# Two edge loops of a graph network on Trainium2: no memsets between the gathers of the additive loop, its turn and sums at later lags; in the attention loop the merge moves to VectorE, a copy to ScalarE, and GpSimd only gathers

## What is computed

```python
# layer 1, "additive": 4 heads of 32 channels
projected = (x @ W).reshape(N, 4, 32)
scores = tanh(projected[row] + projected[col])
scores = einsum('ehc,hc->eh', scores, att)
scores = exp(scores - max(scores, axis=0))
out = segment_sum(projected[row] * scores[:, :, None], col)
out = out / maximum(segment_sum(scores, col), 1e-12)[:, :, None]

# layer 2, "GAT": 2 heads of 128 channels
e = leaky_relu(xl[src] + xr[dst], 0.2)
alpha = einsum('ehd,hd->eh', e, att)
alpha = exp(alpha - segment_max(alpha, dst)[dst])
alpha = alpha / (segment_sum(alpha, dst)[dst] + 1e-16)
out = segment_sum(xl[src] * alpha[..., None], dst).mean(axis=1) + h @ res_W + bias
```

## Time and profile before

| | |
|---|---|
| time, median of 3 runs | 4551.61 us (4547.66 to 4561.69) |
| the profiled execution | 4548.06 us, of which the span is 4546.3 us |
| busy over the span | PE 87%, DVE 63%, ACT 39%, POOL 73% |
| gathers of the additive layer | from 672.23 to 1862.8 us |
| gathers of GAT | from 1981.62 to 3100.7 us |
| granted clock over the span | 0.877 |

### The profile page before, as it was taken

The page is one execution under the profiler, slowest core; times in us unless marked ns, Lnnn a source line. Parts: engine busy times, 40 slices in busy tenths (PEclk is TensorE's granted clock), DMA queues, the critical chain, the costliest instruction groups (busy, mean ns, idle before and its releaser), DMA issues. The chain is left out here.

```text
span 4546.3 us, 91170 instructions
## 1 busy us (share of the span) xinstructions
PE 3966.6 (87%) x22715; PEld 2253.3 (50%) x22818; DVE 2873.2 (63%) x8482; ACT 1768.1 (39%) x4516; POOL 3334.8 (73%) x4366
## 2 busy tenths in 40 slices
PE   2998848889898888679999999996799999999977
PEld 1344434455455555445555554554465656656552
DVE  7997033333333333567677776776788888888859
ACT  3775033444434444343333333333322222222217
POOL 0533238888888888468888888884588888888862
PEclk8999977777767777689898999998899999999999
DMA  2222622222222222044333333331566666666650
GB/s 86 82 83 66 200 76 62 59 59 58 58 59 57 59 59 57 21 148 116 111 111 111 112 111 111 111 111 28 103 103 105 104 104 104 104 105 104 105 102 14
DMA packets 377441, 402.57 MB, mean 89 GB/s; under 512 B 86457, under 2 KB 322502, under 8 KB 377030
## 3 DMA queue, kind: packets, MB, share of 16 engines
q0 software_dynamic: 151904, 198.72, 22.8%
q1 hardware_dynamic: 225382, 202.21, 15.7%
HBM read 312.91 MB, written 87.78 MB: 88 GB/s over the span
## 5 line engine op out<-in xcount | busy, mean ns | idle before, releaser
L1735 POOL DMA_INDIRECT sums<-gathered,idx x606 | 988.9, 1632 | 217.4 <-issue 166.1
L896 POOL DMA_INDIRECT gathered<-table,sources x952 | 917.6, 964 | 169.6 <-issue 134.3
L1597 PE MATMUL bank<-wide 128*128 128x512 bf16 x3533 | 829.2, 379 | 5.6 <-issue 0.2
L2411 ACT ACTIVATE msg<-bank,neg_top 80x512 f32<-80x512 f32 (+1 forms) x404 | 275.9, 683 | 858.1 <-DVE neg_top L2465 842.9
L1597 PEld LDWEIGHTS bank<-wide 128*128 128x128 bf16 x3636 | 347.7, 98 | 364.1 <-issue 1.8
L2463 DVE TENSOR_REDUCE neg_raw<-bank 80x1 f32<-80x512 f32 (+1 forms) x404 | 276.7, 685 | 388.9 <-PE bank L2341 328.5
L896 POOL DMA_INDIRECT wide<-table,sources x464 | 447.9, 965 | 76.9 <-issue 62.3
L1236 POOL TENSOR_TENSOR acc<-acc,msg 128x20 f32 x404 | 172.8, 428 | 350.2 <-issue 188.4
L2320 PE MATMUL bank<-ident,gathered 128*128 128x128 f32 x1360 | 277.9, 322 | 140.8 <-DMA gathered<-table,sources 118.2
L2320 PEld LDWEIGHTS bank<-ident,gathered 128*128 128x128 f32 x1360 | 188.9, 162 | 412.4 <-issue 197.1
L2341 PE MATMUL bank<-zact,att_cells 128*80 128x512 f32 x404 | 319.9, 886 | 0.0
(11 more groups left out here) (413 smaller groups left out, 8006.8 us busy)
## 6 DMA issues: line engine op xcount, KB each, us to landing
zact<-in_src_flat SPq DMA_DIRECT2D x202, 192.0 KB, 3.1
edge_rows<-in_attr_rows SPq DMA_DIRECT2D x202, 128.0 KB
dst_pair<-local_rows SPq DMA_DIRECT2D x177, 128.0 KB
gathered<-table,sources POOLq DMA_INDIRECT x952, 2.6
dst_pair<-local_rows SPq DMA_DIRECT2D x202, 64.0 KB
counts<-wide SPq DMA_DIRECT2D x4, 3000.0 KB
counts<-fm_ab SPq DMA_DIRECT2D x4, 3000.0 KB
fm_ab<-counts SPq DMA_DIRECT2D x4, 3000.0 KB, 11.2
```

Of the source, the lines that this page charges most:

```text
L896: pool.indirect_dma_start(out=g[:, j, :], out_offset=None, in_=table, in_offset=bass.IndirectOffsetOnAxis(ap=mine, axis=0)).then_inc(rows_ ...
L1597: pe.matmul(k.bank[b][:, :], k.split[t.two][:, c, :], k.source_hot[t.two][:, b * CHUNK:(b + 1) * CHUNK], start=first, stop=c == PARTS - 1, ...
L1735: pool.indirect_dma_start(out=k.sums[j], out_offset=bass.IndirectOffsetOnAxis(ap=k.idx[t.slot][:, j:j + 1], axis=0), in_=out_rows(t)[:, j, ...
L2411: act.activation(raised(t), score_bank(t), ACT.Exp, bias=k.neg_top[lanes(t), bass.ds(t.t, 1)], accum_out=k.weight_sum[lanes(t), bass.ds(t. ...
```

## The change

In the additive layer `rest` and its memset go; TensorE's `turn` moves from lag 4 to 5 and its `sums` from 5 to 7, and with them VectorE's `edge_weights` (4 to 5) and ScalarE's `keep_sums` and merge steps (5 to 7). In GAT the four window operations of a tile move from GpSimd to VectorE, as a new last stage at lag 16, all but the last six tiles' `rows` pair, which stays on GpSimd; the copy of the turned weights moves from VectorE to ScalarE, as a new stage at lag 4 in front of `copy_sums`; and window addresses are read four at a time, once every fourth tile, for each of VectorE's two users.

```diff
@@ over_tiles
-            slot = (s_slot - lag) % ring
-            rounds = s_round if s_slot >= lag else s_round - 1
+            slot, back = (s_slot - lag) % ring, (lag - s_slot + ring - 1) // ring
+            rounds = s_round - back if back else s_round
...
-def rest(k, pool, paused, t, j, columns):
-
-    if t.t + j > 0:
-        pool.wait_ge(paused, t.t * SUB + j)
-    pool.memset(columns, 0.0).then_inc(paused, 1)
...
     for j in range(SUB):
         gather_rows(k, pool, table, g, rows_loaded, t, j)
-        rest(k, pool, paused, t, j, k.pause)
@@ WindowMerge
+    def bases_of(self, dve, t, held):
+        if t.slot % BATCH == 0:
+            n = min(BATCH, self.k.tiles - t.t) if isinstance(t.t, int) else BATCH
+            held[:] = window_bases(self.k, dve, t.t, n)
+        return held[t.slot % BATCH]
+
+    def add_tiles_of(self, dve, t, held):
+        if isinstance(t.t, int) and t.t >= self.pooled():
+            return
+        at = self.bases_of(dve, t, held)
+        self.scale_acc(dve, t.t, t.slot, at)
+        self.scale_rows(dve, t.t, t.slot, at)
+        self.add_acc(dve, t.t, at)
+        self.add_rows(dve, t.t, t.slot, at)
@@ beside_gathers
+        if m < self.pooled():
+            return
         if j == 0:
-            pool.wait_ge(self.taken, self.done(m // self.ring, m % self.ring // BATCH))
-            self.scale_rows(pool, m, at)
-        elif j == 1 and m < self.pooled():
-            self.scale_acc(pool, m, at)
+            pool.wait_ge(self.taken, self.done(m // self.ring, slot // BATCH))
+            self.scale_rows(pool, m, slot, at)
         elif j == 2:
-            self.add_rows(pool, m, at)
-        elif j == 3 and m < self.pooled():
-            self.add_acc(pool, m, at)
+            self.add_rows(pool, m, slot, at)
@@ attend, TensorE, additive
-                    over_tiles(pe, k.tiles, [(3, scores), (1, features), (4, turn), (5, sums)], head=3, ring=ring)
+                    over_tiles(pe, k.tiles, [(3, scores), (1, features), (5, turn), (7, sums)], head=3, ring=ring)
@@ attend, ScalarE
+                def copy_weights(t):
+                    act.wait_ge(turned, t.t + 1)
+                    wait_count(act, sums_ready, t.t - 1)
+                    act.copy(k.edge_rows[t.two][:, 0:SUB * cells], weight_bank(t)).then_inc(weight_ready, 1)
...
-                    over_tiles(act, k.tiles, [(3, raise_scores), (1, activate), (5, copy_sums)], head=2, ring=ring)
+                    over_tiles(act, k.tiles, [(3, raise_scores), (1, activate), (4, copy_weights), (5, copy_sums)],
+                               head=2, ring=ring)
...
-                    over_tiles(act, k.tiles, [(3, raise_scores), (1, activate), (5, keep_sums),
-                                              (5, merge_steps)], head=3, ring=ring)
+                    over_tiles(act, k.tiles, [(3, raise_scores), (1, activate), (7, keep_sums),
+                                              (7, merge_steps)], head=3, ring=ring)
@@ attend, VectorE
                 def best_of_nodes(t):
-                    at = window_base(k, dve, t)
+                    at = fold.bases_of(dve, t, top_bases)
...
-                                              (4, best_of_nodes), (4, edge_weights)], head=3, ring=ring)
+                                              (4, best_of_nodes), (16, add_tiles_of)], head=3, ring=ring)
...
-                    over_tiles(dve, k.tiles, [(0, onehots), (3, tops), (4, edge_weights)], head=3, ring=ring)
+                    over_tiles(dve, k.tiles, [(0, onehots), (3, tops), (5, edge_weights)], head=3, ring=ring)
```

More of the change, by code:

```diff
@@ L61 @@
 STRIDE2 = 32
-PAUSE = 280
 def ceil_div(a, b):
@@ L2039, in note, with scale_acc @@
         return dve.tensor_tensor(best, best, top, ALU.max).then_inc(self.best, 1)
-    def scale_acc(self, eng, m, at):
-        half, i = m % self.ring // BATCH, m % BATCH
+    def scale_acc(self, eng, m, slot, at):
+        half, i = slot // BATCH, slot % BATCH
         wait_count(eng, self.acc_added, m)
@@ L2049, in add_acc, with scale_rows, add_rows @@
         w = self.k.acc[:, :, bass.ds(at, WIN)]
[L2050 to L2054, removed]
-        z = self.k.node_sum[:, bass.ds(at, WIN)]
[L2056 to L2061, removed]
-        z = self.k.node_sum[:, bass.ds(at, WIN)]
-        pool.tensor_tensor(z, z, self.row_sums[half][:, i * WIN:(i + 1) * WIN], ALU.add).then_inc(self.rows_added, 1)
+        eng.tensor_tensor(w, w, self.a.partial[:, :, bass.ds(m, 1), :].rearrange("p z t n -> p z (t n)"),
+                          ALU.add).then_inc(self.acc_added, 1)
+    def scale_rows(self, eng, m, slot, at):
+        half, i = slot // BATCH, slot % BATCH
+        wait_count(eng, self.rows_added, m)
+        z = self.k.node_sum[:, bass.ds(at, WIN)]
+        eng.tensor_tensor(z, z, self.row_factors[half][:, i * WIN:(i + 1) * WIN],
+                          ALU.mult).then_inc(self.rows_scaled, 1)
+    def add_rows(self, eng, m, slot, at):
+        half, i = slot // BATCH, slot % BATCH
+        eng.wait_ge(self.rows_scaled, m + 1)
+        z = self.k.node_sum[:, bass.ds(at, WIN)]
+        eng.tensor_tensor(z, z, self.row_sums[half][:, i * WIN:(i + 1) * WIN], ALU.add).then_inc(self.rows_added, 1)
+    def bases_of(self, dve, t, held):
[11 more added lines that the diff above has]
+        self.add_rows(dve, t.t, t.slot, at)
     def pooled(self):
@@ L2184, in tail_takes @@
         for i, at in enumerate(window_bases(k, dve, first, k.tiles - first)):
-            self.scale_acc(dve, first + i, at)
+            self.scale_acc(dve, first + i, (first + i) % self.ring, at)
             self.add_acc(dve, first + i, at)
@@ L2304, in _ @@
                         wait_count(pool, sums_ready, n + 1 - ring)
-                        gather(k, pool, table, rows(t), gathers_begun, rows_loaded, t, paused)
+                        gather(k, pool, table, rows(t), gathers_begun, rows_loaded, t)
             @block.tensor
@@ L2475, in edge_weights, with add_tiles_of @@
                     dve.wait_ge(turned, t.t + 1)
[L2476 to L2479 removed]
+                    if t.slot == 9 and (not isinstance(t.rounds, int) or t.rounds > 0):
+                        dve.wait_ge(kept, t.rounds * ring)
+                    merge.read_turn(dve, t, merge_bank(t))
                     wait_count(dve, sums_ready, t.t - 1)
                     dve.tensor_copy(k.edge_rows[t.two][:, 0:SUB * cells], weight_bank(t)).then_inc(weight_ready, 1)
[L2482 to L2483 removed]
+                    merge.behind_turn(dve, t)
+                top_bases, sum_bases = [], []
+                def add_tiles_of(t):
+                    fold.add_tiles_of(dve, t, sum_bases)
                 def best_of_nodes(t):
[L2486 removed]
+                    at = fold.bases_of(dve, t, top_bases)
                     dve.wait_ge(top_turned, t.t + 1)
```

13 lines of the change are left out of this document (3 added, 10 removed).

## The result

| | before | after |
|---|---|---|
| time, median of 4 runs | 4553.83 us (4547.66 to 4561.69) | 4269.17 us (4265.89 to 4272.35) |
| span of the profiled execution | 4546.3 us | 4264.2 us |
| additive layer, first to last gather | 1189.6 us | 1009.2 us |
| GAT, first to last gather | 1118.2 us | 1010.8 us |

The ratio is 0.9374, 95% interval 0.9357 to 0.9391: 284.7 us less, where 251 were forecast.

A forecast was written before the change was run, and what follows sets the result against it. GpSimd's gathers were taken to pace both loops. 169 us (additive) + 96 (GAT) - 3 (lags) - 3 (GAT's end) - 8 (stalls) = 251 us less, giving 4297 profiled and 4301 for the median; range 4278 to 4385.

The forecast's parts named there:

- What bounds the loops: Additive loop and GAT: GpSimd's gathers set the pace, 1.474 and 1.396 us each, although TensorE looks busier.
- The price of a bare gather: Both loops: 1.265 us an interval, between 1.25 and 1.277, saving 169 us in the additive loop and 96 in GAT.
- The 8 us for stalls in GAT: GAT: VectorE's small margin gets lost whenever TensorE's clock dips, charged at 8 us.
- 3 at GAT's end: End of GAT: tiles 186 to 195 are added on VectorE behind the last steps, half uncovered, 3 us more.
- clean 1.25 us intervals: Both loops: better than forecast, gathers save 181 + 107 us with little lost, down to 4275 us; chance 0.04.
- VectorE's chain: GAT: VectorE's steps with the window operations need 4.8 us a tile, under GpSimd's 5.06 by a little.
- What the lateness hit first: GAT: a late VectorE would first hit TensorE's turn of the maxima, with about 2 us of lateness free.
- Rival 1: GAT: VectorE becomes the bound at 5.2 to 5.4 us a tile, taking 25 to 60 us; 4325 to 4365; chance 0.18.
- Rival 2: Additive loop: stays bound by TensorE's low clock, saving 146 us or half of it; 4325 to 4385; chance 0.10.
- rival 3: Additive loop: TensorE's clock stays down at 7.33 us a tile, 1,481 us, so slower, about 4750; chance 0.05.
- Rival 4: Additive loop: memsets cover something, only GAT's part stays, 4460; chance 0.05 shared with both first two rivals at once.
- The rule against the move: GAT: VectorE's window operations and GpSimd's gathers might lock each other out; at most 31 us by the rows.
- The lags: Additive loop: later lags cost nothing within it but put two more tiles' sums behind the last gather, 3 us more.

The follow-up runs named there:

- experiments 1 to 5: Each half alone (ratios 0.9619, 0.9773), old lags (0.9384), 8-column memsets (0.9405), node_sum pair on GpSimd (0.9477), copy back on VectorE (0.9527) or moved with additive half only (0.9621).
- experiment 5: Changed kernel with the copy of the edge weights back on VectorE: ratio 0.9527; kernel before with the additive half and only the copy moved to ScalarE: 0.9621.
- (6): Changed kernel with VectorE loading one window address at each use through `window_base` instead of four at a time: ratio 0.9660.
- (7): Changed kernel with only one of a tile's four gathers issued and waited for from the ring's second turn on, in both loops: 3989.76 us.
- (4): Changed kernel with GAT's scale and add on node_sum left on GpSimd between the gathers: ratio 0.9477.
- (2): Changed kernel with the additive loop's `turn`, `sums` and their followers back at lags 4 and 5: 4267.71 us, ratio 0.9384.

## Why the prediction was off

**What bounds the loops: right.** GpSimd's pace set both before; each half's gain is its gathers' intervals times their number (experiments 1 to 5).

**The price of a bare gather: the step that failed.** "They take 2072.30 - 1981.62 = 90.7 us for 71 intervals, 1.277 each." There are 72 intervals. The gather at 2072.30 is number 73, the first of the nineteenth tile, which is issued ahead of the first merge operation. GpSimd's count in a window of the kernel before that ends with it (POOL busy, the fifth number in brackets) says so:

```profile
1982.00:2073.00 91.00, 78.14 (x564) 41.53 (x561) 58.48 (x161) 34.27 (x82) 69.06 (x73) 0.88 0.48 132
```

So the mean was 90.7 / 72 = 1.259. Five of the 72 intervals are long, 1.29 to 1.40 us, as the gathers that they begin with take 0.99 to 1.10 us; the others are 1.25 or 1.26. From the false 1.277 I made a "jitter" and took 1.265. The loops ran at 1.2506 and 1.2525. In the additive loop this is 807 x 0.0144 = 11.6 us: -180.4 instead of -169. In GAT the count was off by one too: from 2073.64 to the last gather there are 734 intervals, not 735, of 1.398 us, not 1.396, and the 735 that change begin at 2072.30. 735 x (1.398 - 1.2525) = 106.9, measured 107.4, instead of 96.

**The 8 us for stalls in GAT: not needed.** The second mis-sized term. GpSimd's waits in the changed kernel, 1812 to 2800 us:

```profile
POOL gathered L894 <- issue: 112.1, 368, 0.3
...
POOL gathered L894 <- PE bank L2375: 7.0, 23, 0.3
```

None for TensorE's sums is longer than the 0.30 us gap itself, so none costs anything; what TensorE loses in a dip of its clock it makes up within the ring.

These two make 11.4 + 11.4 + 8 = 30.8 of the 31.1 us between 251 and the spans' 282.1. The rest nearly cancels: the prediction charged 3 us between the loops and 3 at GAT's end, where 3.5 and 6.0 were measured, and the first gather came 3.8 us earlier by chance. Why GAT's end costs 6.0 and not 3 no run isolates. The range's lower end came from the same 1.277: a case at "clean 1.25 us intervals" had 0.04, and it was the one that came true, at 4269 rather than 4275.

**VectorE's chain: right in kind, nearer the edge than forecast.** 4.8 us a tile forecast, 4.98 measured. The window operations took 0.71 instead of 0.6 us, the exposed load 0.11 a step (10.9 us over 100 steps) instead of 0.2. Most of the rest shows between the maximum and the leaky relu, where the prediction changed nothing: 2403.71 - 2401.31 = 2.40 us in the step shown, 2042.04 - 2039.85 = 2.19 in the earlier trace rows, one step each. The margin was 0.03 us a tile, not 0.26. Rival 1 missed by that much: the copy left in place (experiment 5) or addresses read by `window_base` in each step (6) would have made it true. What the lateness hit first at TensorE was not the turn of the maxima, as I wrote, but the one-hot rows.

**Rival 2 and 3, TensorE's low clock: refuted, with their premise.** The clock in the additive loop rose from 0.73 to 0.83, and it holds 1.00 once no gather is waited for (7). Being busy at 1.2 GHz did not keep it low. The two paces that the prediction took from the earlier trace rows are also of two kinds of steps. The one of 7.33 us holds matmuls of the merge, the one of 3.43 does not:

```profile
1330.67 0.71 PE L1801 MATMUL bank<-wide,own 80*128 80x80 f32 x2
```

The mean tile at 2.4 GHz takes 3.60 us (7), and 202 x 7.33 us for rival 3 was too much, by how much no stretch of these runs at 1.2 GHz shows. Rival 4, memsets that cover something, fell with the first view.

**The rule against the move: not met here.** No gather grew beside VectorE's window operations, 0.95 us in GAT with them and without (4); the 0.96 to 0.99 of the kernel before belong to gathers right behind a GpSimd operation. The Trainium skill, "SBUF — State Buffer", section "Who interferes with whom", has VectorE operations with two SBUF inputs and GpSimd's reads of SBUF lock each other out. The same section says that `tensor_tensor`, which the window operations are, was not seen to stall DMAs in its probe, and the prediction left that out. The trace agrees with this second sentence: an indirect gather meets no such lock here.

**The lags: priced at 3 us, nothing that can be told from noise** (2). Between the loops the time moved by 3.5 us, but it moves as much among kernels alike in that part.

## What to carry to other kernels

Where a queue of like instructions paces a loop, a change that cleans it is worth the number of intervals times (old interval - clean interval), as long as the other engines keep up, and the clean interval is to be read off a dozen neighbouring rows, not off a long stretch divided by a counted number: here a miscount by one in 72, with a charge for stalls that no row asked for, left the measured time outside the range. Work moved to another engine needs that engine's chain of waits below the pace, not its busy share: VectorE at 80% busy had 0.6% to spare, and which of its waits could go stood one step up the chain, in the order of ScalarE's list. And loads of addresses into registers should be batched where they stand in such a chain, since a load of one took 0.31 us and a load of four 0.35, and what the reading function adds behind each load has to be looked at as well.

## What the runs showed of the chip

- Back to back, an indirect gather of 128 rows mostly takes 0.94 to 0.95 us and the next begins 0.30 us behind its end, for rows of 512 bytes and 1 KB alike. Behind another GpSimd operation the gap is 0.15 to 0.18 us, and the gather takes 0.95 us behind a memset and 0.96 to 0.99 behind the window operations. A memset of 128x8 fp16 elements takes 0.13 us, one of 128x280 0.36.
- A load of window addresses takes VectorE's queue 0.31 us for one and 0.35 for four (medians). With what stands behind the load VectorE idles 0.69 us (mean of 89) in front of `scale_acc` with `window_base` and one address, 0.44 (mean of 25) with `window_bases` and four.
- In a loop that waits for gathers TensorE's granted clock averages 0.83; the same loop with three of four gathers left out has 1.00, and its tile takes 3.60 us instead of 5.0.
